# Four-layer gated model on one core: products of ones in seven more places where TensorE waits, and an earlier start of layer four's score stream

## What is computed

```python
for each layer l:
    x = x + tanh(g_xattn[l]) * xattn_l(x, ctx)
    x = x + tanh(g_ffn[l])   * ffn_l(norm(x))
# layer one:   scores, layer norm, softmax; FFN of 8 experts, top 2, relu
# layer two:   16 heads of 16 with a causal mask, online maxima; FFN with ternary
#              weights, inputs quantised to 8 bits per token, Hadamard transforms
# layer three: adjacency = the 76 largest scores of each row, mixed with gamma;
#              FFN = a shared expert of 1024 plus top 2 of 8 routed experts
# layer four:  32 query heads, 8 key heads of width 8; FFN = a shared expert of 704
#              plus top 2 of 8 routed experts of 176
```

## Time and profile before

| | |
|---|---|
| median of 3 runs | 852.88 us |
| the runs | 851.64, 852.88, 859.55 us |
| the profiled execution | 859.66 us |
| its span in the trace | 857.9 us |
| mean granted clock of TensorE | 0.908 of full |
| PE busy | 715.5 us, 83% |
| PE weight loads | 473.9 us, 55% |
| DVE busy | 546.8 us, 64% |
| ACT busy | 348.9 us, 41% |
| POOL busy | 206.9 us, 24% |

### The profile page before, as it was taken

The page is one execution under the profiler, slowest core; times in us unless marked ns, Lnnn a source line. Parts: engine busy times, 40 slices in busy tenths (PEclk is TensorE's granted clock), DMA queues, the critical chain, the costliest instruction groups (busy, mean ns, idle before and its releaser), DMA issues. The chain is left out here.

```text
span 857.9 us, 13857 instructions
## 1 busy us (share of the span) xinstructions
PE 715.5 (83%) x4399; PEld 473.9 (55%) x4399; DVE 546.8 (64%) x1655; ACT 348.9 (41%) x617; POOL 206.9 (24%) x299
## 2 busy tenths in 40 slices
PE   9999987878877745968786998976888889998995
PEld 4543556656764632646665776743233226776774
DVE  6787888886755965577675453445876856513554
ACT  2653555555437611512013413425468784212220
POOL 0003782001000220011413451542233220251331
PEclk9999999998888966879998799998589999999998
DMA  6993420400000400000133050012000033032314
GB/s 201 337 204 96 140 87 8 140 11 2 3 1 1 148 1 0 1 1 1 54 116 118 32 185 26 22 53 70 1 2 3 1 124 82 26 111 61 104 66 166
DMA packets 55487, 60.17 MB, mean 70 GB/s; under 512 B 13832, under 2 KB 48729, under 8 KB 55417
## 3 DMA queue, kind: packets, MB, share of 16 engines
q1 hardware_dynamic: 50328, 45.96, 18.8%
q0 software_dynamic: 4848, 13.28, 4.4%
q10 hardware_dynamic: 240, 0.05, 0.0%
HBM read 34.86 MB, written 24.20 MB: 69 GB/s over the span
## 5 line engine op out<-in xcount | busy, mean ns | idle before, releaser
L1856 ACT ACTIVATE arenas<-psum 128x512 f32<-128x512 f32 (+5 forms) x81 | 55.4, 703 | 59.7 <-PE psum L1095 40.5
L3053 DVE TENSOR_REDUCE arenas<-psum 128x2 f32<-128x512 f32 x96 | 62.1, 685 | 19.6 <-PE psum L1652 18.3
L1095 PE MATMUL psum<-conb,shared 128*128 128x128 bf16 (+2 forms) x512 | 41.7, 240 | 19.4 <-POOL shared L909 9.2
L907 POOL TENSOR_SCALAR arenas<-arenas,small 128x1024 f32<-128x1024 f32 x8 | 9.0, 1121 | 202.4 <-DVE small L2798 202.4
L1095 PEld LDWEIGHTS psum<-conb,shared 128*128 128x128 bf16 (+2 forms) x512 | 36.5, 126 | 27.6 <-issue 16.1
L921 POOL DMA_INDIRECT experts_l<-shared,small x30 | 29.2, 975 | 82.4 <-ACT shared L2148 70.5
L1543 PE MATMUL psum<-arenas,early 128*128 128x256 f32 (+1 forms) x192 | 43.9, 383 | 1.3 <-issue 1.0
L1856 ACT ACTIVATE late<-psum 128x512 f32<-128x512 f32 (+1 forms) x51 | 24.5, 504 | 48.2 <-PE psum L1095 48.1
L1095 PE MATMUL psum<-con,early 128*128 128x128 f32 (+1 forms) x188 | 32.5, 294 | 11.7 <-DVE early L2296 4.0
L2192 ACT ACTIVATE early<-psum 128x1024 f32<-128x1024 f32 x32 | 32.4, 1036 | 23.5 <-PE psum L1669 23.2
L3018 DVE TENSOR_TENSOR shared<-shared,psum 128x128 f32<-128x128 f32 x30 | 8.5, 286 | 51.3 <-PE psum L1605 29.2
(11 more groups left out here) (435 smaller groups left out, 1819.2 us busy)
## 6 DMA issues: line engine op xcount, KB each, us to landing
sorted_l<-late SPq DMA_DIRECT2D x3, 1920.0 KB, 17.8
early<-sorted_l SPq DMA_DIRECT2D x6, 645.0 KB, 5.8
early<-in_L_ffn_sw SPq DMA_DIRECT2D x3, 1024.0 KB, 9.0
late<-sorted_l SPq DMA_DIRECT2D x23, 129.0 KB, 2.0
sorted_l<-late SPq DMA_DIRECT2D x1, 2944.0 KB, 24.0
early<-in_L_ffn_We_gate_up SPq DMA_DIRECT2D x2, 1408.0 KB
early<-in_L_ffn_expert_w SPq DMA_DIRECT2D x2, 1024.0 KB, 6.9
early<-in_L_ffn_w SPq DMA_DIRECT2D x1, 2048.0 KB, 8.3
```

The costliest lines, as they stand in the source:

```text
L907: pool.tensor_scalar(ha[s][:, rows], ha[s][:, rows], c2[s][:, t:t + 1], ROUND, ALU.mult, ALU.add)
L1095: last = pe.transpose(v[0:parts, at:at + k], src, idn[0:k, 0:k])
L1856: act.activation(dst, view(v), ACT.Copy, scale=scale).then_inc(f.drained(i, key), 1)
L3053: dve.tensor_reduce(nm, q3d(f.slot(0, ("max", w, k)), 2, S), X, ALU.max, negate=True)\
```

## The change

It adds calls of `kept_busy` at seven places, 91 products in all: in `scores1` three times two and once three for each batch pair (18); 13 ahead of the second pair's turned queries; 12 and 3 around the last turn of layer two's attention; 6 and 8 ahead of the first pair's two input turns in `ffn1`; 14 ahead of the second pair's rows in `ffn2`; 5, 8 and 4 ahead of the second to fourth step of `attention3`. It also moves the shift rows of unit one behind the first exponentials' scores and the first piece of unit two's maxima, frees the wait for the banks of one stage of bank 5, puts an exponential on a small tile on ACT ahead of the last move of columns (which brings its table load there), lets DVE begin with the returned expert rows at step 6 of a unit's maxima and not at step 2, and keeps the pieces of the top-76 search out of three steps of the routing.

```diff
--- before.py
+++ after.py
@@ -1380,8 +1380,11 @@
 
                 for name, s, *k in max_order1():
                     if name == "max":
+                        if s == 0 and k[0] > 8:
+                            kept_busy(pl["l1x"]["V"], i, ("pv", 0), 2)
                         max1(i, s, *k)
                     elif name == "shT":
+                        kept_busy(pl["l1x"]["V"], i, ("pv", 0), 3)
                         shift1(i, s)
                     elif name != "qsT":
                         turn_column1(i, name, s, *k)
@@ -1421,11 +1424,14 @@
             turn_heads(0, 1)
             queries1(1, 1)
             project(0, 1)
+            kept_busy(pl["l1x"]["V"], 1, ("pv", 0), 13)
             queries_turned1(1)
             key_values1(1, 1)
             scores1(1)
             tokens1(1, 1)
+            kept_busy(pl["prep1b"]["A"], 0, ("tern", 0, 0), 12)
             turn_heads(1, 1)
+            kept_busy(pl["prep1b"]["A"], 0, ("tern", 0, 0), 3)
             project(1, 1)
 
             banks_free("prep1b", 0)
@@ -1474,6 +1480,8 @@
                 fa, fb, fc = (pl["l1f"][g] for g in "ABC")
                 banks_free("l1f", i)
                 for s in range(2):
+                    if i == 0:
+                        kept_busy(fb, i, ("g", 0, 0, 0), 6 + 2 * s)
                     pe.wait_ge(xq_ready.sem, xq_ready.count(2 * i + s))
                     turn_x(fa, i, s, ("qT", s), xq[s], identb, BF16)
                     yield
@@ -1551,7 +1559,7 @@
 
                 if i == 0:
                     yield from steps(MIX)
-                    kept_busy(fa, i, ("xT", 0), 8)
+                kept_busy(fa, i, ("xT", 0), 8 + 6 * i)
                 for s in range(2):
                     pe.wait_ge(xn_ready["l2f"].sem, xn_ready["l2f"].count(2 * i + s))
                     turn(fa, i, ("xT", s), [(P, c * S + t * P, rows2[i][:, s * T + t, c * P:(c + 1) * P])
@@ -1719,13 +1727,16 @@
                             turn_columns3(1, COLUMNS_AT[k])
                         yield
                     yield
-                    shift3(w)
+                    if w == 0:
+                        shift3(0)
                     yield
 
             def maxima3():
                 for w in range(2, UNITS):
                     for k in range(16):
                         max3(w, k)
+                        if (w, k) == (2, 0):
+                            shift3(1)
                         yield
                         if k == SHIFT_AT and w > 2:
                             shift3(w - 1)
@@ -1734,10 +1745,13 @@
 
             def attention3():
 
-                banks_free("l3x", 0)
+
+                banks_free("l3x", 0, besides=(5,))
                 maxima = maxima3()
                 for g in range(8 * UNITS):
                     w, m = g // 8, g % 8
+                    if 0 < g < 4:
+                        kept_busy(pl["l3x"]["V"], 0, ("tok", 0), (5, 8, 4)[g - 1])
                     if m == 0:
                         pe.wait_ge(shift_in3[w % 2].sem, shift_in3[w % 2].count(w // 2))
                     exp3(w, m)
@@ -2166,6 +2180,9 @@
                     yield
                 yield from steps(10)
                 for k in range(0, 16, 2):
+                    if k == 14:
+
+                        act.activation(c4_all, gt[:, 0:2 * T], ACT.Exp)
                     if k in COLUMNS_AT:
                         move_columns(1, COLUMNS_AT[k])
                     yield
@@ -3130,7 +3147,7 @@
                             shift_turned3(w - 1)
                         if k == 2 and w >= 4:
                             reciprocals3(w - 4)
-                        if k >= 2:
+                        if k >= 6:
                             next(beside, None)
                     alone(beside)
                 shift_turned3(UNITS - 1)
@@ -3241,8 +3258,10 @@
 
             def with_largest(stage):
 
+
+                routing = [s * HC + j for s, j in (ROUTE, CHOOSE, PLACE)]
                 for k, _ in enumerate(stage):
-                    if k >= 2 * MIX:
+                    if k >= 2 * MIX and k - 2 * MIX not in routing:
                         next(largest, None)
                     yield
                 alone(largest)
```

## The result

The changed kernel took 850.2 us (median of 20, 843.69 to 859.9), the one before 854.5 us (20, 849.19 to 864.32). The ratio is 0.994, 95% interval 0.9918 to 0.9963: 4 to 5 us gained, where 12 were forecast. The time lies in the forecast's range; the gain of over 1%, which it took as the likelier case, didn't come.

What follows compares the result with a forecast made beforehand. The prediction took TensorE at half its clock, after idle gaps, to set the pace in low stretches. Terms 0 - 2.5 - 2.1 - 0.9 - 3.5 - 3 + 0 = -12.0 us took 852.88 to 841 us, range 830 to 855.

Steps and rivals of the forecast that it cites:

- Part 1: Layer two's score maxima: bursts cost the first pair 0.9 us, net 0.9 lost in the second offset by 1.8; sum 0.
- Part 2: Thirteen ones ahead of layer two's second-pair queries fill PE's idle time and keep the clock full: -2.5 us.
- Part 3: End of layer two's attention: twelve and three ones let turn and projection run at full clock: -2.1 us.
- Part 4: First gates of layer two's FFN: six and eight ones spare three gate and up pairs the half clock: -0.9 us.
- Part 5: Fourteen ones before the second pair's rows in layer three's FFN shorten a 14.5 us PE-bound stretch: -3.5 us.
- Part 6: Head of layer four, four edits at once: -3 us, between -7 and +4.
- (b): Layer four's head: returned expert rows from step 6, not 2, spare DVE a DMA wait; worth up to 1.4 us.
- (a): Layer four's head: earlier ACT table load, and first exponential's scores no longer behind unit one's shift rows; net -0.5 us.
- (c): Layer four's head: seventeen ones in idle time, 7.7 us at half clock or 3.6 at full, partly delaying scores.
- (d): Layer four's head: if the clock rises near 600, DVE becomes the bound; 7 of its 8.8 us idle could go.
- The clock falls again: Rival: behind each burst the fall only moves, gains shrink to shifts; 851 us, chance 0.23.
- Transposes don't hold the clock: Rival: the clock falls during transposes behind the ones, so parts 2, 3 and 5 give 0; 849 us, chance 0.08.

Runs made afterwards that it cites:

- f12: e1 without the ones at layer two's queries, the end of its attention and its first FFN gates; 859.31 us, ratio 0.997 to the kernel before.
- e2: The kernel before with only the four edits of layer four; 858.86 us, ratio 1.0037.
- e1: The changed kernel without its four edits of layer four, the routing edit kept; 843.64 us, ratio 0.9844 to the kernel before.
- f11: e1 without the fourteen ones in layer three's FFN; 850.63 us, ratio 0.9872 to the kernel before.
- g3: The same kernel as e1, run again in session four; 855.03 us, ratio 0.9895 to the kernel before.
- g4: g3 without the routing edit on the search's pieces, same session; 855.99 us, ratio 0.9914 to the kernel before.
- f10: e1 without the routing edit on the search's pieces, in session three; 856.49 us, ratio 0.9943 to the kernel before.
- e5: The changed kernel with the returned expert rows added from step 2 again; 842.27 us, ratio 0.9847 to the kernel before.
- e6: e1 with the returned expert rows added from step 6; 845.23 us, ratio 0.988 to the kernel before.
- g2: The changed kernel with returned rows from step 6 in unit two only, from step 2 in unit three; session four, 852.82 us, ratio 0.9871.
- g1: The changed kernel itself, run again in session four; 860.73 us, ratio 0.9976 to the kernel before.
- e7: e1 with layer four's moved shift rows and earlier table load; 842.15 us, ratio 0.984 to the kernel before.
- e3: The changed kernel without the 17 ones of layer four; 847.47 us, ratio 0.9875 to the kernel before.
- e8: e1 with the 17 ones of layer four; 841.83 us, ratio 0.9835 to the kernel before.

## Why the prediction was only in part right

- **Part 1, maxima of layer two** (0; -2.1 to +3.8): measured in the changed trace +0.69 in the first pair and -0.53 - 0.97 + 0.31 in the second, -0.5. The mechanism and both signs held.
- **Part 2, thirteen** (-2.5; -1.2 to -3.2): DVE's copy is 2.4 us earlier, but the program was 0.6 us behind when the ones began. From there to ACT's move at 202.45 it gained 3.6 us. The mechanism held, the size was too small. In f12, without the ones, the lead fell by 0.4. One trace is a rough yardstick here: e2, whose program is that of before up to layer four, gained 2.7 at the same place, since its low stretch lasted 3.4 us and not 10.3.
- **Part 3** (-2.1): from the start of the turn to DVE's addition 5.62 us before, 3.37 after, -2.25, as forecast.
- **Part 4** (-0.9): the lead grew from 7.1 us at the first ternary move to 7.8 at the place of 270.06, near the forecast. Then the clock fell from 276 to 283.5, the lead was 5.1 at the place of 290, and 6.7 at that of 351. The term priced a stretch that goes; it moved on. In e1 it was shorter (278.5 to 281.9), and the lead 7.9 at 351. f12 against f11 shows parts 2 to 4 together: 8.7 us on one chip and the fourteen's part besides, where 5.5 were forecast.
- **Part 5** (-3.5; 0 to -5.6): the lead grew from 9.1 to 11.3 us at the next places, -2.2; the clock held for 6 us and fell at 464, a case that the prediction weighed. But f11, without the fourteen, gained 2.8 of the 3.3 us over the whole stage, so they are worth some 0.5 us. The step that was wrong is the stretch of 14.5 us taken for granted without them. Over the whole time nothing was resolved.
- **DVE's pieces of the search** (0 within 1): the local effect was missed. The lead grew from 6.7 to 10.5 us between layer three's first products and 403 in the changed trace, from 6.7 to 10.6 in g3, and from 2.4 to 2.5 in g4, which lacks the edit. PE waited 2.7 us less for DVE in the three waits shown. The forecast looked for who waits for the moved pieces, and not for who waited behind them: DVE's L2947 and L2819, for which PE stood. But by the place of 439 the whole change had 7.7 us left, g3 7.7 and g4 2.5, so that 0.9 of the edit's gain remained, and g3 and g4 end 1 us apart, within the term's own margin. f10 and f11 end 5.9 us apart, though their traces are level at 439 (7.7 and 7.8 us ahead). What the edit is worth to the end stays open.
- **Part 6** (-3; -7 to +4), the step that failed. Its (b), "that is worth up to 1.4", priced the DMA wait that goes. The wait did go, and up to the place of 630 the head gained 1.6 us, and 4.1 in e2. But beginning at step 6 of 16 leaves the rows' steps ten places and not fourteen, and presses the norm's small steps between the last maxima, in unit three too, where no DMA was late. PE then waits for DVE at a place where the clock had been full, and the clock fell for 24 us with PE busy 22.44 of them, at half speed: 9.4 us lost. e5 (whole change, rows early: no stretch, 0.9847), e6 (late rows alone: stretch) and g2 against g1 (unit three alone: 7.9 us) show that the late rows of unit three are the cause. That the PE wait of 1.12 us is what tips the clock is supported by its standing in all six traces with the stretch and in no other; no run removed that wait alone, so it isn't shown.
- The price of the late rows over the whole time differs by session: 3.1 us from e7 to e6 (which lacks the moved shift rows too), 7.9 from g2 to g1. The executions of the whole change (around 844 and around 852 us), e3 (841.3 to 845.9 at clocks of 0.924 to 0.932, and 849.1 to 850.6 at 0.918) and e6 (842.6 to 846.3 and 849.4 to 851.4) suggest that not every execution has the stretch. Only the profiled ones have windows, so this is an inference from their mean clocks.
- Its (a), -0.5, and (c) and (d), the ones: e7 and e8 have ratios of 0.984 and 0.9835, and e1 0.9844 in another session; e5 and e7 differ by 0.1 us in one session. Over the whole time they bring nothing that can be told. Between the places of 591 and 630 the traces contradict each other: with ones e5 gains 1.6 us more than e7, and the whole change 3.5 less than e3. "DVE becomes the bound" held, and so nearly all of (d)'s -7 was never there: e5's clock rose and its time didn't fall. DVE's idle time under a slow PE was taken for what a fast PE would free.
- **The rivals.** "The clock falls again" happened, but in a place where no ones stood and through an edit on DVE; the prediction had tied it to the bursts. It also happened in layer two's FFN (276 to 283.5). "Transposes don't hold the clock" is refuted for parts 2 and 3: 187 to 200 and 240 to 249 stayed at 1.00, where turns follow the ones, with the products L1371 and L1354 among them. The Trainium skill, page "TensorE: Matmul & The Clock Gate", section "Part 4: PE-mode transpose", says that the full clock doesn't engage for transpose mode, which doesn't count as busy in the same way. No run here tests transposes without products beside them.
- **The sum.** Ahead of layer four -9 was forecast and -12.6 measured in the trace, with the search's pieces in it. For layer four -3 was forecast, and the trace has -1.6 in the head, +9.4 in the late stretch and -1.9 behind it, -6.7 in all. That the measured time lies in the range is in part luck: parts that gave more than forecast made up for a loss of 9.4 us, where part 6 had +4 as its worst end. Parts 1 to 5 with the routing edit took 843.64 us in e1, 11.9 less than before; that this is the 12 forecast for the whole is luck too. On the chip of session four the same kernel gained 6.4 us (g3). There its lead fell from 11.4 us behind layer three's first products (461.67) to 7.9 at the last column move (583.56). Its trace has a low stretch from 552.5 to 559.3 in between, which e1's hasn't. What makes it was not tried. (A slip in the working: 91 ones at 0.45 us are 41 us, not 39; nothing rests on it.)

The versions with the lowest ratios are e1, e5, e7 and e8 (0.9835 to 0.9847) in their sessions, and g2 and g3 in theirs. Among them these runs can't choose.

## What to carry to other kernels

Ones in a wait of TensorE paid where a stretch bound by PE followed and the burst was shorter than the wait, as in parts 2 and 3. Part 5 met both conditions and gave some 0.5 us, since the kernel without its ones wasn't slow in the same place for as long: what ones are worth is told by the same kernel without them, not by the old trace. Where DVE was nearly full behind them, a faster clock bought next to nothing. A step moved on another engine is to be priced by the products that it will hold up, at every place where the loop's rule applies and not only where it was needed, and the clock that those products lose is part of the price.

## What the runs showed of the hardware

- The same program falls into low stretches at different places from one execution and chip to another. g3's trace has one from 552.5 to 559.3 us and e1's, of the same kernel, has none there. Against the kernel before that kernel gave 0.9844 on one chip and 0.9895 on another, and the whole change 0.994 and 0.9976. Differences of 0.5% between ratios of two sessions say nothing here.
- A fall at a place where PE waited 1.12 us lasted 24 us with PE busy 93%: being busy with real products of this kind at half speed didn't end it (0.50 from 624.5 to 648.5).
- Thirteen products of 128x512 took 2.97 us at the full clock and fourteen 3.18, 0.21 us more.
